# First attention stage: the additive band mask moves from identity products on TensorE into a VectorE add that copies the scores to SBUF

## The chip, the core and the metric

The kernel runs on one core of one Trainium2 chip. The metric is the device time of one execution of the whole program in microseconds (us), as the median of the runs. The program is a six-layer decoder (two attention-like mixers, two cross attentions, a mixture of experts, a binarised feed-forward); only its first layer is touched here.

## The reference, cut to what matters

The touched layer is a windowed self attention with rotary positions, 8 batches of 256 tokens, 16 heads of 64. Every query sees only keys at a distance of at most 64.

```
Q = (x @ Wq).reshape(Bx, Tx, H, D).transpose(0, 2, 1, 3)
K = (x @ Wk).reshape(Bx, Tx, H, D).transpose(0, 2, 1, 3)
V = (x @ Wv).reshape(Bx, Tx, H, D).transpose(0, 2, 1, 3)
Q = Q * cos + rotate_half(Q) * sin
K = K * cos + rotate_half(K) * sin
scores = jnp.einsum('bhqd,bhkd->bhqk', Q, K) / jnp.sqrt(jnp.float32(D))
w = Tx // 4
allowed = jnp.abs(idx[:, None] - idx[None, :]) <= w
scores = jnp.where(allowed[None, None], scores, -jnp.inf)
attn = jax.nn.softmax(scores, axis=-1)
out = jnp.einsum('bhqk,bhkd->bhqd', attn, V)
return out.transpose(0, 2, 1, 3).reshape(Bx, Tx, H * D) @ Wo
...
x = _layernorm(x + _L0_attn_ref(x, L0_attn_Wq, L0_attn_Wk, L0_attn_Wv, L0_attn_Wo), axis=-1)
```

## The kernel before

The layer is the function `window_attention`. Nothing schedules it: each engine has a written-out list of instructions, and semaphores tie the lists together. All engines work in order within their own list, so the position of a step in a list decides what is queued behind it.

A batch is worked in four **groups** (`g` = 0 to 3) of four heads (`GH` = 4). Because of the window, the 128 queries of a tile `t` need only `SPAN` = 192 keys, so one head's scores for both tiles are 2 x 192 = 384 columns of one PSUM bank, `s_bank[i]`. There is one such bank for each head of a group, and one name for all of them in the profile: `wa_scores`.

What a group's work is, by engine:

- TensorE, in `score` (lines 639 to 658): four products of a bf16 identity with the bf16 `band` (L649) write 0 or -1e30 into the 384 columns of each bank, and sixteen products of rotated q and k (L655) accumulate onto that.
- VectorE, in `maximum` (L468): for each of the four heads one reduction over 384 columns of PSUM, which gives the negated row maximum.
- ScalarE, in `exponential` (L383): two exponentials per head, of 192 columns each, which read the same PSUM bank and write `probs` to SBUF.
- TensorE turns the probabilities (`turn_probs`, L667), for two heads at a time; one such pair is a unit `u`. ScalarE takes the high half out of PSUM (`wa_pth`, L394) and VectorE the rest (`wa_ptl`, L509); TensorE weighs the values (`weigh`, L685); VectorE normalises (L494, L502).

Beside this a group carries part of the **next** batch or of the previous one:

- All groups but those of the last batch project q and k for the next batch (`project`, L596) into `s_bank[0]` and `s_bank[1]`, which VectorE reads with the cosines and sines (L462, L463) before GpSimd adds (L342, L343). So group `g+1`'s scores wait in `score` until VectorE has read the projections of group `g` (`rope_read`).
- Groups 0 and 3 (**value groups** below) make two value products each for the next batch in the single bank `m_bank` (L617, `wa_misc`). ScalarE copies the first out after its eight exponentials (L399), VectorE takes the rest (L474, `value_low`), and only then may TensorE start the second (semaphore `misc_free`).
- Groups 1 and 2 (**mix groups**) do the output projection of the previous batch there (L634) and its residual and statistics on VectorE (L482, L145 to L150).
- At the end of group 3 VectorE also applies the layer norm (L159) and splits the next input (L452).

The first batch has no previous batch and the last one has no next, so batch 0's groups 1 and 2 have no mix, and the last batch's groups have neither values nor projections. That leaves 14 value groups: two in each of batches 0 to 6.

VectorE's list in a group is: four maxima, normalise the previous unit, the value rest or the residual, `wa_ptl` of the first unit, the second value rest, four reads of the projections, `wa_ptl` of the second unit, normalise. TensorE's is: weigh the previous unit, value product or mix, turn the first unit, second value product, project, turn, weigh, turn the heads (L627), next group's scores.

Of the kernel before, what the change touches and what calls it, by code (L numbers as in the profile page):

```python
# [21 lines left out]
BF16 = mybir.dt.bfloat16  # L22
I32 = mybir.dt.int32
ALU = mybir.AluOpType
ACT = mybir.ActivationFunctionType
AX = mybir.AxisListType

P = 128
# [3 lines left out]
TPB = SEQ // P  # L32
# [77 lines left out]
def identity(pool, tile, made, done):  # L110

    pool.memset(tile[:], 0.0).then_inc(made, 1)
    pool.wait_ge(made, done)
    return pool.affine_select(out=tile[:], in_=tile[:], compare_op=ALU.not_equal, fill=1.0, base=0,
                              pattern=[[-1, P]], channel_multiplier=1)
# [47 lines left out]
def first(b):  # L163

    return isinstance(b, int) and b == 0
# [6 lines left out]
WINDOW = SEQ // 4  # L172
SPAN = P + WINDOW
# [3 lines left out]
GROUPS = 4  # L177
# [32 lines left out]
def window_attention(nc, x_dram, xt_dram, wqkv_dram, wo_dram, rope_dram, ident, half, X, next_loads):  # L210
    with ExitStack() as ctx:
        def sb(name, shape, dt=F32):
            return ctx.enter_context(nc.sbuf_tensor("wa_" + name, shape, dt))

        def sem(name):
            sems.append(nc.alloc_semaphore("wa_" + name))
            return sems[-1]
# [14 lines left out]
        vh = [sb(f"vh{k}", [P, TPB, HEADS, HD + 1], F16) for k in range(2)]  # L232
        vl = [sb(f"vl{k}", [P, TPB, HEADS, HD + 1], F16) for k in range(2)]
        probs = [sb(f"probs{k}", [P, 2, SEQ]) for k in range(4)]
        minus_top = sb("minus_top", [P, 2, GH, 2])
        pth = [sb(f"pth{k}", [P, 2 * SEQ], F16) for k in range(4)]
        ptl = [sb(f"ptl{k}", [P, 2 * SEQ], F16) for k in range(4)]
        inv = sb("inv", [P, 2, TPB, 2])
        heads_out = sb("heads_out", [P, TPB, HEADS, HD])
        heads_t = [sb(f"heads_t{k}", [P, HEADS // 2, SEQ]) for k in range(2)]  # L240
        ident_bf = sb("ident_bf", [P, P], BF16)
        band = sb("band", [P, TPB, SPAN], BF16)

        s_bank = [ctx.enter_context(nc.psum_tensor(f"wa_scores{k}", [P, 2 * SEQ], F32)) for k in range(GH)]
        t_bank = [ctx.enter_context(nc.psum_tensor(f"wa_turned{k}", [P, 512], F32)) for k in range(2)]
# [19 lines left out]
        misc_free = sem("misc_free")  # L265
        v_high = sem("v_high")
        scores = sem("scores")
        maxed = sem("maxed")
        exped = sem("exped")
        probs_t = sem("probs_t")  # L270
# [50 lines left out]
        @block.gpsimd  # L321
        def _(pool):
            identity(pool, ident, consts, 1).then_inc(consts, 1)
            identity(pool, ident_bf, consts, 3).then_inc(consts, 1)
            pool.memset(half[:], -0.5).then_inc(consts, 1)
            pool.memset(band[:], 0.0).then_inc(consts, 1)
            pool.wait_ge(consts, 6)

            for t, base in ((0, 0), (1, P - WINDOW)):
                n = 6 + 2 * t  # L330
                pool.affine_select(out=band[:, t], in_=band[:, t], compare_op=ALU.is_ge, fill=NEG,
                                   base=base + WINDOW, pattern=[[-1, SPAN]], channel_multiplier=1).then_inc(consts, 1)
                pool.wait_ge(consts, n + 1)
                pool.affine_select(out=band[:, t], in_=band[:, t], compare_op=ALU.is_ge, fill=NEG,
                                   base=WINDOW - base, pattern=[[1, SPAN]], channel_multiplier=-1).then_inc(consts, 1)

            def rotate(b, par, g, w):

                n = rope_count(b, g, w)
                pool.wait_ge(rope_read, n + 1)  # L340
                out = turned[w][par]
                pool.tensor_tensor(out[:, g, 0], by_cos[w][:, 0], by_sin[w][:, 1], ALU.add)  # L342
                pool.tensor_tensor(out[:, g, 1], by_cos[w][:, 1], by_sin[w][:, 0], ALU.add).then_inc(rope_done, 1)  # L343

            def batch(b, par, before=True, after=True):
                for g in range(GROUPS):
                    if after:
                        for w in range(2):
                            rotate(b + 1, 1 - par, g, w)
                    if before and g == 2:  # L350
                        norm.root(pool, b - 1, 0)
                        norm.root(pool, b - 1, 1)

            for g in range(GROUPS):
                for w in range(2):
                    rotate(0, 0, g, w)
            pool.wait_ge(w_low, 6)
            batch(0, 0, before=False)
            with pool.Fori(0, BATCH // 2 - 1) as i:
                batch(2 * i + 1, 1)  # L360
                batch(2 * i + 2, 0)
            batch(BATCH - 1, 1, after=False)
            norm.root(pool, BATCH - 1, 0)
            norm.root(pool, BATCH - 1, 1)

        @block.scalar
        def _(act):
# [8 lines left out]
            def exponential(b, g, i):  # L376
                n = GH * (GROUPS * b + g) + i
                u, h = 2 * g + i // 2, i % 2
                act.wait_ge(maxed, n + 1)
                if not (first(b) and u < 2):  # L380
                    act.wait_ge(probs_t, b * 16 + 2 * u - 2)
                for t in range(TPB):
                    ins = act.activation(probs[2 * (u % 2) + t][:, h, t * WINDOW:t * WINDOW + SPAN],  # L383
                                         s_bank[i][:, t * SPAN:(t + 1) * SPAN], ACT.Exp,
                                         bias=minus_top[:, g % 2, i, t:t + 1])
                ins.then_inc(exped, 1)

# [55 lines left out]
        def _(dve):  # L443
# [21 lines left out]
            def maximum(b, g, i):  # L465
                n = GH * (GROUPS * b + g) + i
                dve.wait_ge(scores, GROUPS * b + g + 1)
                dve.tensor_reduce(minus_top[:, g % 2, i], s_bank[i][:, 0:2 * SPAN].rearrange("p (t s) -> p t s", t=2),  # L468
                                  AX.X, ALU.max, negate=True).then_inc(maxed, 1)

            def value_low(b, par, i, n):
                t, c = divmod(i, 2)
# [75 lines left out]
            split_w(0)  # L548
            split_w(1)
            dve.wait_ge(rope_loaded, 32)  # L550
            for g in range(GROUPS):
                rope(0, g, 0)
                rope(0, g, 1)
                if g < 2:
                    split_w(g + 2)
                elif g == 2:
                    split_w(4)
                    split_w(5)
# [18 lines left out]
        def _(pe):  # L577
            def project(b, par, g, w):

                n = rope_count(b, g, w)  # L580
                if w == 0:
                    pe.wait_ge(x_low, b + 1)
                    if first(b):
                        pe.wait_ge(w_low, g + 1)
                if first(b):
                    if g >= 2:
                        pe.wait_ge(rope_read, n - 3)
                else:
                    pe.wait_ge(exped, GH * (GROUPS * (b - 1) + g) + w + 1)
                bank = rope_bank(b, g, w)  # L590
                for a in range(2):
                    cols = slice(g * 512 + w * 256 + a * P, g * 512 + w * 256 + (a + 1) * P)
                    m = 0
                    for k in range(KT_):
                        for weight, x in ((wh, xh), (wh, xl), (wl, xh)):
                            ins = pe.matmul(bank[:, a * SEQ:(a + 1) * SEQ], weight[:, k, cols], x[:, par, k],  # L596
                                            start=(m == 0), stop=(m == 3 * KT_ - 1))
                            m += 1
                ins.then_inc(projected, 1)
# [38 lines left out]
            def score(b, par, g):  # L638

                pe.wait_ge(rope_done, rope_count(b, g, 1) + 1)  # L640
                if not (first(b) and g == 0):
                    pe.wait_ge(exped, GH * (GROUPS * b + g))
                if isinstance(b, int) and b == BATCH - 1:
                    pe.wait_ge(rope_read, 2 * GROUPS * BATCH)
                else:
                    pe.wait_ge(rope_read, 2 * GROUPS * (b + 1) + 2 * g)
                q, k = turned[0][par], turned[1][par]
                for i in range(GH):
                    pe.matmul(s_bank[i][:, 0:2 * SPAN], ident_bf[:], band[:].rearrange("p t s -> p (t s)"),  # L649
                              start=True, stop=False, skip_group_check=True)  # L650
                for part in range(2):
                    for t in range(TPB):
                        for i in range(GH):
                            rows = slice(FREQS * i, FREQS * (i + 1))
                            ins = pe.matmul(s_bank[i][:, t * SPAN:(t + 1) * SPAN], q[rows, g, part, t * P:(t + 1) * P],  # L655
                                            k[rows, g, part, t * WINDOW:t * WINDOW + SPAN], start=False,
                                            stop=(part == 1 and t == TPB - 1), skip_group_check=True)
                ins.then_inc(scores, 1)

            def turn_probs(b, u):  # L660
# [54 lines left out]
                    elif after:  # L715
                        score(b + 1, 1 - par, 0)

            pe.wait_ge(consts, 10)
            for g in range(GROUPS):
                project(0, 0, g, 0)  # L720
                project(0, 0, g, 1)
# [2079 lines left out]
```

## Time and profile before

| | before |
|---|---|
| median of 3 runs | 1324.53 us |
| the 3 runs | 1319.22, 1324.74, 1324.53 us |
| the profiled execution | 1319.36 us |
| its span | 1317.6 us |
| TensorE busy | 1104.7 us, 84% of the span |
| VectorE busy | 940.1 us, 71% |
| ScalarE busy | 702.1 us, 53% |
| GpSimd busy | 389.0 us, 30% |
| mean granted TensorE clock | 0.927 of 2.4 GHz |

The busy times cover the whole program. The touched layer fills the first 442 us. In it the profile's rows are to be read by group: a group begins when VectorE starts the first of its four L468 reductions.

### The profile page before, as it was taken

How to read it: one execution, taken by the hardware profiler on the slowest of the kernel's cores; microseconds unless marked ns; L12 is line 12 of the kernel's file. 1: busy time of each engine (PE TensorE's matmuls, PEld its weight loads, DVE VectorE, ACT ScalarE, POOL GpSimd, SP SyncE). 2: the span in 40 equal slices, each digit the busy share in tenths (PEclk: the TensorE clock that was granted, in tenths of full speed). 3: DMA queues.
4: the chain of work that ended last, by engine and by line, in shares of the span. 5: the costliest groups of instructions: out<-in, count | busy, mean ns of one | idle time of the engine just before them, and what ended most of it. 6: DMA issues, size and time to landing. Idle time of an engine off the chain costs nothing. (4 is left out here: it accounts for less than half of the span.)

```text
span 1317.6 us, 29952 instructions
## 1 busy us (share of the span) xinstructions
PE 1104.7 (84%) x10635; PEld 895.0 (68%) x10635; DVE 940.1 (71%) x2221; ACT 702.1 (53%) x1458; POOL 389.0 (30%) x538
## 2 busy tenths in 40 slices
PE   5899989989988699996449999489999569999696
PEld 3578768768777477775337777378888447777485
DVE  7676766767765279885847884569998528898487
ACT  2444444444444155553727776267778525655484
POOL 5122222212220155552050000413421125555232
PEclk9999999999999799997559999699999769999799
DMA  6000000100000500002443531300100000000011
GB/s 255 1 10 2 10 10 1 68 3 1 2 1 2 182 13 22 21 8 119 192 146 114 209 118 40 123 21 17 32 8 9 0 24 20 14 21 8 33 49 48
DMA packets 34064, 65.26 MB, mean 50 GB/s; under 512 B 7590, under 2 KB 23334, under 8 KB 30886
## 3 DMA queue, kind: packets, MB, share of 16 engines
q1 hardware_dynamic: 32422, 59.62, 12.8%
q0 software_dynamic: 1536, 4.20, 0.9%
q8 instruction: 70, 1.15, 0.4%
q14 instruction: 36, 0.29, 0.1%
HBM read 43.03 MB, written 12.39 MB: 42 GB/s over the span
## 5 line engine op out<-in xcount | busy, mean ns | idle before, releaser
L925 POOL TENSOR_TENSOR ca_z<-ca_z,ca_top 128x308 f32<-128x308 f32 x128 | 92.5, 723 | 135.4 <-DVE ca_top L1054 135.1
L383 ACT ACTIVATE wa_probs<-wa_scores,wa_minus_top 128x192 f32<-128x192 f32 x256 | 83.1, 436 | 68.2 <-DVE wa_minus_top L468 68.2
L394 ACT ACTIVATE wa_pth<-wa_turned 128x384 f16<-128x384 f32 x128 | 58.2, 505 | 96.9 <-PE wa_turned L667 96.9
L997 ACT ACTIVATE ca_pth<-ca_turned 77x512 f16<-77x512 f32 x128 | 75.8, 592 | 61.5 <-PE ca_turned L1181 60.9
L342 POOL TENSOR_TENSOR wa_q<-wa_by_cos,wa_by_sin 128x256 f32<-128x256 f32 x32 | 23.4, 730 | 284.2 <-DVE wa_by_sin L463 284.2
L1181 PE MATMUL ca_turned<-ident,ca_probs 128*77 128x128 f32 x512 | 85.0, 290 | 20.8 <-ACT ca_probs L989 19.8
L1172 PE MATMUL ca_scores<-ca_km,ca_q 128*128 128x308 f32 x256 | 91.0, 439 | 6.0 <-ACT ca_q L970 5.7
L468 DVE TENSOR_REDUCE wa_minus_top<-wa_scores 128x2 f32<-128x384 f32 x128 | 62.4, 550 | 37.7 <-PE wa_scores L655 37.7
L1059 DVE SCALAR_TENSOR_TENSOR ca_ptl<-ca_turned,ca_pth 77x512 f16<-77x512 f32 x128 | 86.7, 677 | 2.6 <-ACT ca_pth L997 2.6
L989 ACT ACTIVATE ca_probs<-ca_z 128x308 f32<-128x308 f32 x128 | 58.2, 454 | 44.8 <-POOL ca_z L925 43.8
L596 PE MATMUL wa_scores<-wa_xh,wa_wh 128*128 128x256 f16 x256 | 70.9, 277 | 10.8 <-DVE wa_wl L447 8.9
L1181 PEld LDWEIGHTS ca_turned<-ident,ca_probs 128*77 128x77 f32 x512 | 56.7, 150 | 26.6 <-ACT ca_probs L989 23.0
L667 PE MATMUL wa_turned<-ident,wa_probs 128*128 128x128 f32 x512 | 67.8, 274 | 8.0 <-DVE wa_ptl L509 5.4
L596 PE MATMUL wa_scores<-wa_xl,wa_wh 128*128 128x256 f16 x256 | 70.9, 277 | 0.0
L596 PE MATMUL wa_scores<-wa_xh,wa_wl 128*128 128x256 f16 x256 | 70.9, 277 | 0.0
L2357 PE MATMUL re_g<-re_convh,re_w_gh 128*128 128x256 f16 x256 | 69.8, 273 | 1.2 <-DVE re_convl L2252 1.2
L509 DVE SCALAR_TENSOR_TENSOR wa_ptl<-wa_turned,wa_pth 128x384 f16<-128x384 f32 x128 | 65.0, 549 | 7.9 <-ACT wa_pth L394 7.9
L2357 PE MATMUL re_g<-re_convl,re_w_gh 128*128 128x256 f16 x256 | 69.8, 273 | 0.0
L2357 PE MATMUL re_g<-re_convh,re_w_gl 128*128 128x256 f16 x256 | 69.8, 273 | 0.0
L2341 PE MATMUL re_in<-re_xt,re_w_in 128*128 128x256 f32 x256 | 61.8, 403 | 9.0 <-ACT re_xt L2122 9.0
L667 PEld LDWEIGHTS wa_turned<-ident,wa_probs 128*128 128x128 f32 x512 | 58.2, 141 | 15.2 <-issue 6.3
L2341 PEld LDWEIGHTS re_in<-re_xt,re_w_in 128*128 128x128 f32 x256 | 51.1, 202 | 18.8 <-issue 7.2
(325 smaller groups left out, 3613.0 us busy)
## 6 DMA issues: line engine op xcount, KB each, us to landing
ex_stage<-in_ew SPq DMA_DIRECT2D x16, 1024.0 KB, 6.9
slots<-slots_zeros SPq DMA_DIRECT2D x10, 512.0 KB, 5.8
ca_xs<-tokens SPq DMA_DIRECT2D x16, 256.0 KB, 2.3
ex_xe<-slots SPq DMA_DIRECT2D x11, 320.0 KB, 3.2
slots<-ex_y SPq DMA_DIRECT2D x9, 320.0 KB
wa_x_stage<-in_xt SPq DMA_DIRECT2D x8, 256.0 KB, 3.0
tokens<-in_x SPq DMA_DIRECT2D x1, 2048.0 KB, 14.8
ca_w<-in_xw SPq DMA_DIRECT2D x2, 1024.0 KB, 5.7
```

The lines of the kernel that those rows point to most:

```text
L383: ins = act.activation(probs[2 * (u % 2) + t][:, h, t * WINDOW:t * WINDOW + SPAN], s_bank[i][:, t * SPAN:(t + 1) * SPAN], ACT.Exp, bias=mi ...
L468: dve.tensor_reduce(minus_top[:, g % 2, i], s_bank[i][:, 0:2 * SPAN].rearrange("p (t s) -> p t s", t=2), AX.X, ALU.max, negate=True).then_ ...
L509: dve.scalar_tensor_tensor(out=spans(ptl[k][:]), in0=spans(t_bank[h][:]), scalar=PSCALE, in1=spans(pth[k][:]), op0=ALU.mult, op1=ALU.subtr ...
L596: ins = pe.matmul(bank[:, a * SEQ:(a + 1) * SEQ], weight[:, k, cols], x[:, par, k], start=(m == 0), stop=(m == 3 * KT_ - 1))
L667: ins = pe.transpose(t_bank[h][:, j * SEQ + t * P:j * SEQ + (t + 1) * P], probs[2 * (u % 2) + t][:, h, j * P:(j + 1) * P], ident[:])
L925: pool.tensor_tensor(z[k][:], z[k][:], top[:, k].unsqueeze(2).broadcast_to((P, UH, CTX)), ALU.subtract).then_inc(shift, 1)
L997: act.activation(pth[k][0:CTX], t_bank[k][0:CTX], ACT.Copy, scale=PSCALE).then_inc(probs_high, 1)
L1059: dve.scalar_tensor_tensor(out=ptl[k][0:CTX], in0=t_bank[k][0:CTX], scalar=PSCALE, in1=pth[k][0:CTX], op0=ALU.mult, op1=ALU.subtract).then ...
L1172: pe.matmul(s_bank[c % 2][:, 0:UH * CTX], q[par][:, g, t * P:(t + 1) * P], km[par][:, g, h:h + UH].rearrange("p h k -> p (h k)"), start=Tr ...
L1181: ins = pe.transpose(t_bank[k][0:CTX, h * P:(h + 1) * P], probs[k][:, h], ident[:])
L2341: ins = pe.matmul(i_bank[s % 2][:, k], w_in[:, g, m * P:(m + 1) * P], xt[:, g], start=(g == 0), stop=(g == KT_ - 1))
L2357: ins = pe.matmul(g_bank[m][:, k], w[:, j, cols], x[par][:, j], start=(n == 0), stop=(n == 3 * HT - 1))
```

## The change

The band is no longer written into PSUM by TensorE. The four identity products of each group are gone, and with them the bf16 identity. The band is now an f32 tile. VectorE adds it to each head's 384 score columns while it copies them to a new SBUF tile `z[i]`, one for each head of a group, and the reduction reads `z[i]`. ScalarE's exponentials read `z[i]` as well. A new semaphore `masked` counts the adds: the reduction waits for its own add, and TensorE's reuse of the score banks waits for the add, where it used to wait for the exponential. The add waits until the previous group's exponential of the same head has read `z[i]`. TensorE's sixteen score products go by tile and then by part, where they went by part and then by tile; the first part now starts the accumulation.

```diff
+        z = [sb(f"z{i}", [P, TPB, SPAN]) for i in range(GH)]
...
-        ident_bf = sb("ident_bf", [P, P], BF16)
-        band = sb("band", [P, TPB, SPAN], BF16)
+        band = sb("band", [P, TPB, SPAN])
...
                     ins = act.activation(probs[2 * (u % 2) + t][:, h, t * WINDOW:t * WINDOW + SPAN],
-                                         s_bank[i][:, t * SPAN:(t + 1) * SPAN], ACT.Exp,
+                                         z[i][:, t], ACT.Exp,
                                          bias=minus_top[:, g % 2, i, t:t + 1])
...
             def maximum(b, g, i):
                 n = GH * (GROUPS * b + g) + i
                 dve.wait_ge(scores, GROUPS * b + g + 1)
-                dve.tensor_reduce(minus_top[:, g % 2, i], s_bank[i][:, 0:2 * SPAN].rearrange("p (t s) -> p t s", t=2),
-                                  AX.X, ALU.max, negate=True).then_inc(maxed, 1)
+                if not (first(b) and g == 0):
+                    dve.wait_ge(exped, n - GH + 1)
+                dve.tensor_tensor(z[i][:], s_bank[i][:, 0:2 * SPAN].rearrange("p (t s) -> p t s", t=2), band[:],
+                                  ALU.add).then_inc(masked, 1)
+                dve.wait_ge(masked, n + 1)
+                dve.tensor_reduce(minus_top[:, g % 2, i], z[i][:], AX.X, ALU.max, negate=True).then_inc(maxed, 1)
...
-                    pe.wait_ge(exped, GH * (GROUPS * (b - 1) + g) + w + 1)
+                    pe.wait_ge(masked, GH * (GROUPS * (b - 1) + g) + w + 1)
...
-                    pe.wait_ge(exped, GH * (GROUPS * b + g))
+                    pe.wait_ge(masked, GH * (GROUPS * b + g))
...
-                for i in range(GH):
-                    pe.matmul(s_bank[i][:, 0:2 * SPAN], ident_bf[:], band[:].rearrange("p t s -> p (t s)"),
-                              start=True, stop=False, skip_group_check=True)
-                for part in range(2):
-                    for t in range(TPB):
+                for t in range(TPB):
+                    for part in range(2):
                         for i in range(GH):
                             rows = slice(FREQS * i, FREQS * (i + 1))
                             ins = pe.matmul(s_bank[i][:, t * SPAN:(t + 1) * SPAN], q[rows, g, part, t * P:(t + 1) * P],
-                                            k[rows, g, part, t * WINDOW:t * WINDOW + SPAN], start=False,
-                                            stop=(part == 1 and t == TPB - 1), skip_group_check=True)
+                                            k[rows, g, part, t * WINDOW:t * WINDOW + SPAN],
+                                            start=(part == 0), stop=(part == 1))
```

The rest of the diff renumbers the semaphore that counts the constants.

The order of VectorE (DVE) in batch 0, group 3, a value group, before. A row is a line of the kernel, the operation, its output and inputs, and the semaphores that it waits for; `wa_minus_top` is the negated maximum, `wa_vl` the value rest.

```order
L468 TENSOR_REDUCE wa_minus_top<-wa_scores 128x2 [waits wa_scores] x4
L494 RECIPROCAL wa_inv<-wa_out 128x4 [waits wa_normed,wa_weighted]
L502 TENSOR_TENSOR wa_heads_out<-wa_out,wa_inv 128x2x128 [waits wa_inverted]
L474 SCALAR_TENSOR_TENSOR wa_vl<-wa_misc,wa_vh 128x8x64 [waits wa_v_high]
L509 SCALAR_TENSOR_TENSOR wa_ptl<-wa_turned,wa_pth 128x2x192 [waits wa_probs_high] x2
```

The same place in the changed kernel; the first two rows stand four times in turn.

```order
L470 TENSOR_TENSOR wa_z<-wa_scores,wa_band 128x384 [waits wa_exped,wa_scores]
L473 TENSOR_REDUCE wa_minus_top<-wa_z 128x2 [waits wa_masked]
...
L498 RECIPROCAL wa_inv<-wa_out 128x4 [waits wa_normed,wa_weighted]
L506 TENSOR_TENSOR wa_heads_out<-wa_out,wa_inv 128x2x128 [waits wa_inverted]
L478 SCALAR_TENSOR_TENSOR wa_vl<-wa_misc,wa_vh 128x8x64 [waits wa_v_high]
L513 SCALAR_TENSOR_TENSOR wa_ptl<-wa_turned,wa_pth 128x2x192 [waits wa_probs_high] x2
```

Four instructions have become eight, each reduction behind a wait for the add ahead of it, and all that follows stands behind them.

The order of TensorE (PE) at the end of a group of batch 0, before: the turned heads, the scores of the next group, and the first product of `weigh`.

```order
L627 MATMUL wa_misc<-ident,wa_heads_out 128x128 x3
L649 MATMUL wa_scores<-wa_band,wa_ident_bf 128x384 [waits wa_rope_read,wa_exped,wa_rope_done]
L649 MATMUL wa_scores<-wa_band,wa_ident_bf 128x384 x3
L655 MATMUL wa_scores<-wa_k,wa_q 128x192 x16
L685 MATMUL wa_out<-wa_vh,wa_pth 128x65 [waits wa_normed,wa_probs_low]
```

The same place in the changed kernel.

```order
L632 MATMUL wa_misc<-ident,wa_heads_out 128x128 x3
L657 MATMUL wa_scores<-wa_k,wa_q 128x192 [waits wa_rope_read,wa_masked,wa_rope_done]
L657 MATMUL wa_scores<-wa_k,wa_q 128x192 x15
L687 MATMUL wa_out<-wa_vh,wa_pth 128x65 [waits wa_normed,wa_probs_low]
```

Four products are gone from every group, and the first score product carries their waits.

## Rows read from the trace of the kernel before

**Rows 1.** Windows of a batch's groups: us; busy PE, PEld, DVE, ACT, POOL; clock; DMA.

```profile
201.10:213.20 12.10, 12.10 (x149) 10.67 (x148) 8.45 (x22) 4.94 (x13) 2.78 (x4) 1.00 0.01 3
...
225.31:238.17 12.86, 11.34 (x145) 8.77 (x144) 9.98 (x22) 6.43 (x16) 2.79 (x4) 1.00 0.01 1
238.17:251.12 12.95, 11.34 (x145) 8.77 (x143) 8.74 (x19) 5.96 (x15) 2.79 (x4) 1.00 0.49 172
```

**Rows 2.** Timeline of TensorE: start, duration, operation, count, idle time before.

```profile
201.71 3.70 PE L634 MATMUL wa_misc<-wa_wo,wa_heads_t 128*128 128x256 f32 x16
210.81 0.81 PE L649 MATMUL wa_scores<-wa_band,wa_ident_bf 128*128 128x384 bf16 x4
211.55 1.58 PE L655 MATMUL wa_scores<-wa_k,wa_q 32*128 32x192 f32 x32
227.21 1.04 PE L667 MATMUL wa_turned<-ident,wa_probs 128*128 128x128 f32 x8
229.77 0.39 PE L617 MATMUL wa_misc<-wa_wh,wa_xh 128*128 128x512 f16 x1 [1.52 <-DVE wa_vl L474]
```

**Rows 3.** Timeline of VectorE, a mix group and a value group.

```profile
201.10 1.95 DVE L468 TENSOR_REDUCE wa_minus_top<-wa_scores 128x2 f32<-128x384 f32 x4 [1.42 <-PE wa_scores L655]
206.03 0.43 DVE L145 BATCH_NORM_STATS2 wa_stats<-wa_res 128x6 f32<-128x256 f32 x1
206.50 0.18 DVE L148 BATCH_NORM_AGGREGATE wa_mv<-wa_stats 128x2 f32<-128x6 f32 x1
...
225.31 1.95 DVE L468 TENSOR_REDUCE wa_minus_top<-wa_scores 128x2 f32<-128x384 f32 x4 [1.42 <-PE wa_scores L655]
...
229.02 0.69 DVE L474 SCALAR_TENSOR_TENSOR wa_vl<-wa_misc,wa_vh 128x512 f16<-128x512 f32 x1 [1.21 <-ACT wa_vh L399]
...
237.32 0.68 DVE L452 SCALAR_TENSOR_TENSOR wa_xl<-wa_x_stage,wa_xh 128x512 f16<-128x512 f32 x1
```

**Rows 4.** Timeline of ScalarE in the same value group.

```profile
225.90 2.60 ACT L383 ACTIVATE wa_probs<-wa_scores,wa_minus_top 128x192 f32<-128x192 f32 x8 [2.19 <-DVE wa_minus_top L468]
228.34 0.65 ACT L399 ACTIVATE wa_vh<-wa_misc 128x512 f16<-128x512 f32 x1
```

**Rows 5.** Groups of instructions by line: shapes, count, busy us, mean ns, idle before.

```profile
L468 DVE TENSOR_REDUCE wa_minus_top<-wa_scores 128x2 f32<-128x384 f32 x128 | 62.4, 550 | 37.7 <-PE wa_scores L655 37.7
L509 DVE SCALAR_TENSOR_TENSOR wa_ptl<-wa_turned,wa_pth 128x384 f16<-128x384 f32 x128 | 65.0, 549 | 7.9 <-ACT wa_pth L394 7.9
...
L1054 DVE TENSOR_REDUCE ca_top<-ca_z 128x4 f32<-128x308 f32 x128 | 58.8, 459 | 0.1
L1048 DVE TENSOR_TENSOR ca_z<-ca_scores,ca_limit 128x308 f32<-128x308 f32 x64 | 30.4, 475 | 19.9 <-PE ca_scores L1172 17.5 <-ACT ca_probs L989 1.4 <-issue 0.3
```

**Rows 6.** Timeline of VectorE in batch 0 and in the last batch.

```profile
54.17 1.95 DVE L468 TENSOR_REDUCE wa_minus_top<-wa_scores 128x2 f32<-128x384 f32 x4 [1.06 <-PE wa_scores L655]
57.77 1.02 DVE L509 SCALAR_TENSOR_TENSOR wa_ptl<-wa_turned,wa_pth 128x384 f16<-128x384 f32 x2 [1.10 <-ACT wa_pth L394]
...
389.65 1.95 DVE L468 TENSOR_REDUCE wa_minus_top<-wa_scores 128x2 f32<-128x384 f32 x4 [0.85 <-PE wa_scores L655]
393.26 1.02 DVE L509 SCALAR_TENSOR_TENSOR wa_ptl<-wa_turned,wa_pth 128x384 f16<-128x384 f32 x2 [1.10 <-ACT wa_pth L394]
```

**Rows 7.** Windows around changes of the granted clock, columns as in rows 1.

```profile
34.00:38.00 4.00, 1.49 (x7) 0.53 (x8) 1.39 (x2) 0.90 (x2) 0.00 (x0) 1.00 0.00 0
...
426.50:430.00 3.50, 1.66 (x30) 1.22 (x28) 1.82 (x7) 0.96 (x2) 0.00 (x0) 0.99 0.00 0
430.00:433.30 3.30, 3.02 (x7) 2.48 (x8) 0.00 (x0) 0.23 (x1) 0.00 (x0) 0.50 0.00 0
453.80:457.20 3.40, 1.30 (x4) 0.68 (x4) 3.00 (x6) 0.26 (x1) 0.04 (x1) 1.00 1.09 381
457.20:464.00 6.80, 5.59 (x21) 4.79 (x22) 2.19 (x5) 2.86 (x7) 2.06 (x3) 0.50 0.64 221
```

**Rows 8.** Timeline of TensorE: the last batch's first mix.

```profile
430.28 5.23 PE L634 MATMUL wa_misc<-wa_wo,wa_heads_t 128*128 128x256 f32 x16 [0.69 <-ACT wa_heads_t L404]
```

More of the change, by code:

```diff
@@ L267, in window_attention @@
         scores = sem("scores")
+        masked = sem("masked")
         maxed = sem("maxed")
@@ L323, in _ @@
             identity(pool, ident, consts, 1).then_inc(consts, 1)
-            identity(pool, ident_bf, consts, 3).then_inc(consts, 1)
             pool.memset(half[:], -0.5).then_inc(consts, 1)
             pool.memset(band[:], 0.0).then_inc(consts, 1)
-            pool.wait_ge(consts, 6)
+            pool.wait_ge(consts, 4)
             for t, base in ((0, 0), (1, P - WINDOW)):
-                n = 6 + 2 * t
+                n = 4 + 2 * t
                 pool.affine_select(out=band[:, t], in_=band[:, t], compare_op=ALU.is_ge, fill=NEG,
@@ L550, in _ @@
             dve.wait_ge(rope_loaded, 32)
+            dve.wait_ge(consts, 8)
             for g in range(GROUPS):
@@ L716, in batch @@
                         score(b + 1, 1 - par, 0)
-            pe.wait_ge(consts, 10)
+            pe.wait_ge(consts, 2)
             for g in range(GROUPS):
```

## The prediction, on record before the result was known

> **What bounds the kernel now.** I read four views: the windows of one batch's groups, the timelines of TensorE, VectorE and ScalarE inside them, the groups of instructions by line for prices, and windows where the granted clock changes. The windows show which engine has room: in a mix group TensorE is busy 12.10 of 12.10 us and VectorE 8.45, in the value groups TensorE 11.34 of 12.86 and 12.95 us, VectorE 9.98 and 8.74 [rows 1]. The middle row dots a second mix group, of 12.11 us. So a batch takes 50.02 us; mix groups are bound by TensorE alone, while value groups contain one wait: TensorE stands 1.52 us ahead of the second value product until VectorE has taken the value rest [rows 2]. What ends last there is a chain over three engines: four maxima, eight exponentials, value copy, value rest, second value product. VectorE starts its maxima at 225.31, the exponentials start at 225.90, the value copy at 228.34, the rest at 229.02, the second product at 229.77 [rows 2 to 4]. Whatever the change saves in a mix group is real; whatever lengthens the maxima in a value group is real too.
>
> **What is removed.** Four identity products per group: from the start of the first to the start of the score products, 211.55 - 210.81 = 0.74 us [rows 2]. In every group they stand directly ahead of the scores, with nothing beside them on TensorE, so the scores come 0.74 us sooner wherever TensorE is late. There are 32 groups, so at most 32 x 0.74 = 23.7 us. The exponential's hold on the score banks goes as well; since the exponentials end at 225.90 + 2.60 = 228.50 and the next scores are ready at 238.17 [rows 1, 4], that is worth nothing. The reordering of the sixteen score products changes neither their number nor their banks' rotation: nothing.
>
> **What is added on VectorE.** Four adds of 128x384 per group from PSUM and SBUF. The trace has the same shape with such operands: L509, 549 ns, while L1048 with 308 columns takes 475 [rows 5]. I take 0.55. The four reductions now follow a wait each. Before, they started (1.95 - 0.55) / 3 = 0.467 us apart [rows 3]; a reduction behind an add of its own cannot overlap it. An instruction that waits for its predecessor's result started 206.50 - 206.03 - 0.43 = 0.04 us after its end [rows 3]. One head thus costs 0.55 + 0.04 + 0.467 = 1.06 us, four 4.23, against 4 x 0.467 = 1.87: VectorE has 2.36 us more per group. Bounds: from below 2 x 0.40 per head (384 columns in the pitch that the rows leave after some 0.07 of start), if the pair overlapped fully, 3.2 in all; from above 2 x 0.55 + 2 x 0.04 = 1.18 per head, 4.7 in all. I take 4.23, since the dependence is in the code and the gap in the rows.
>
> The reduction now reads SBUF. The trace has one from SBUF: L1054, 459 ns for 308 columns; 76 columns more at about 1.04 ns (0.40 us / 384) make 538, against 550 from PSUM [rows 5]. So 0.01 us, which I leave out. The Trainium skill (page "VectorE: DVE Perf Modes", section on the TRN2 errata) gives a VectorE operation 58 cycles of fixed cost from SBUF and 120 from PSUM, which would be 65 ns less per reduction. By that rule the value groups' delay below would be about 0.26 us shorter, some 4 us over the stage; the trace's two reductions don't bear it out. ScalarE's exponentials from SBUF I cost like those from PSUM: only the last pair is on the chain.
>
> **Mix groups (12, plus the last batch's two).** The mix itself keeps TensorE busy for 3.70 us [rows 2] while the maxima run, and the first unit's exponentials are out before it ends. What comes later on VectorE (residual, `wa_ptl`) TensorE needs only behind both projections. VectorE's 8.45 + 2.36 = 10.8 us fit in 12.10 - 0.74 = 11.36 [rows 1]. Each is 0.74 us shorter. Cover gone: were VectorE's list another 0.55 us longer, the next scores would wait for its projection reads, and the gain would shrink by all that goes beyond.
>
> **Value groups (14).** The fourth maximum comes at 3 x 1.057 + 0.59 + 0.55 = 4.31 us after the group's start. ScalarE was behind its eight exponentials before and is now fed by the maxima: the last pair starts at 4.35, and at a pitch of (228.34 - 225.90) / 8 = 0.305 us the value copy starts at 4.96, where it was 228.34 - 225.31 = 3.03 [rows 4]. Everything behind it (value rest, second value product, project, turn, weigh, heads) shifts by 1.93 us as one piece. Less 0.74 the next scores come 1.19 us later. In group 3 VectorE itself is later still: its list ends with norm and split, 237.32 + 0.61 = 237.93, only 0.24 ahead of 238.17 [rows 1, 3]. It gets the full 1.93, so the period grows by 1.93 - 0.24 = 1.69. Its 0.61 is 0.68 less the overlap of 0.07 that such operations have. Group 0 has no such tail and grows by 1.2. A steady batch: 1.2 + 1.7 - 2 x 0.74 = +1.4 us.
>
> **The ends.** In batch 0's groups 1 and 2 and the last batch's group 0, without mix, `wa_ptl` starts 3.60 us after the group, directly behind ScalarE's exponentials [rows 6]; it shifts by 1.93 too, and after the earlier scores each group grows by about 1.1. Batch 0: -0.74 (first scores) + 1.2 + 2 x 1.1 + 1.5 = +4.1. Last batch: +1.2, two mix groups at 0.5 - 0.74 = -0.24 each, and +1.9 in group 3, which has no scores to win from: +2.6. Batch 6 has no split, so its group 3 gives 0.5 back. Sum: 4.1 + 6 x 1.4 - 0.5 + 2.6 = **+14.6 us**.
>
> **The clock.** In a value group TensorE's standing time grows. The first turn started 1.90 us after the group and took 1.04, the second value product came at 4.46 [rows 2]; that product now comes at 6.39. Of the 4.5 us between, the turns, now one by one behind the exponentials of each head, keep TensorE busy for 1.04 to 1.2. The rows show what the granted clock did around such stretches: after 1.66 busy of 3.50 us it went to 0.50 for 3.3 us, after 1.30 of 3.40 to 0.50 for 6.8 us, while after 1.49 of 4.00 at 34 us it stayed at 1.00 [rows 7]. In a value group before, only 1.52 us in one piece were idle and the clock stayed 1.00 [rows 1]. The price: the last batch's mix took 5.23 us where the low clock covered 3.0 of it, and 3.70 at the high one: 1.5 us [rows 2, 8]. A whole covered stretch of 3.3 us costs half of it, 1.65; one of 6.8 us with 5.59 busy costs 2.8 [rows 7]. I take 11 of the 14 value groups, eight at 1.65 and three at 2.8, which is 21.6, less 4 for the groups 3 where VectorE is 0.5 us later than TensorE anyway: **+17 us**. Bounds: 0, and 14 x 2.8 = 39. The Trainium skill warns of this pattern (page "TensorE: Matmul & The Clock Gate", section "HAM oscillation"): waits between bursts of products throttle the array again in each turn of a loop. By that rule every value group would pay, by the rows above 14 x 1.65 = 23; it speaks against this change.
>
> **Sum.** 1319.4 + 14.6 + 17 = 1351.0 against the profiled execution. The runs of before lie in two places, 1319.2 and 1324.6, and their median is 5.2 above the profiled one; I add half of that, 2.6: **1353.6 us**.
>
> **Rivals.**
> (A) The clock holds, as in the row at 34 us: only the +14.6, 1336.6. For it: that row, and the clock of 1.00 all through rows 1. Against: twice in rows 7 it fell after stretches no emptier than these.
> (B) The clock falls in every value group and stays low for the longer time: 1322 + 14.6 + 39 = 1376. For it: the row of 6.8 us. Against: behind the gap come 24 dense products, and the row of 3.3 us had such work.
> (C) Faster. VectorE's add and reduction overlap. The delay of the value copy is 3 times the head's cost less 1.24; gain and loss of a steady batch cancel when that delay is about 1.2, so when a head costs 0.81 us. Below it the mix groups' 0.74 wins; with the value groups' wait hidden as well the whole 23.7 us come back, 1322 - 23.7 = 1298. For it: 0.40 us of streaming per instruction. Against: the `masked` wait between them, and 0.04 us seen after such waits.
> (D) No change: both sides cancel, at 0.81 us per head and a clock that holds, 1324.
>
> **How the numbers follow.** Forecast 0.53, A 0.25, B 0.09, C 0.05, D 0.08. The forecast's own range is 1344 to 1364 (the clock term from 8 to 27 within its bounds). For 8 in 10 I take in A and stop short of B and C: 1331 to 1370. About 0.5% (6.6 us) is what a measurement can tell. Faster has C's 0.05, within 0.5% D's 0.08 and a little of A, 0.1 in all, and slower the rest, 0.85.
>
> **What would show it.** Right: adds of 0.55 us and a pitch of 1.06 per head; value rest 5.6 us after the group's start; TensorE's idle ahead of the second value product grown from 1.5 towards 2.9; mix groups of 11.4 us; windows of 0.50 clock between 60 and 430 us, which did not exist. Wrong: a head's pitch under 0.9, a clock of 1.00 throughout (then A), scores that wait for the projection reads in mix groups (then more than B), or another time behind the first layer.

## The result, and the profile after

The changed kernel takes 1359.74 us (median of 4 runs, 1359.42 to 1359.81) against 1321.88 us before (median of 4, 1316.64 to 1324.74). The ratio is 1.0291, with a 95% interval of 1.0252 to 1.0329: slower by 2.9%. The forecast was 1353.6 us in a range of 1331 to 1370.

The windows of one batch show where it went. They answer to [rows 1]; columns are the same: the window, then busy TensorE, its weight loads, VectorE, ScalarE, GpSimd, the granted clock, DMA. The first two are mix groups, the last two the value groups 3 and 0.

```profile
223.31:234.76 11.45, 11.45 (x147) 10.31 (x143) 10.57 (x25) 5.42 (x13) 2.79 (x4) 1.00 0.01 1
234.76:246.22 11.46, 11.46 (x147) 10.32 (x143) 10.57 (x25) 5.42 (x13) 3.17 (x5) 1.00 0.01 1
246.22:263.44 17.22, 14.10 (x153) 9.63 (x150) 12.17 (x25) 7.03 (x16) 3.44 (x6) 0.80 0.01 2
263.44:280.29 16.85, 13.43 (x133) 9.01 (x130) 11.01 (x24) 6.57 (x15) 2.79 (x4) 0.80 0.37 132
```

Mix groups went from 12.10 to 11.45 us, with TensorE still busy throughout; VectorE's work rose by 2.1 us in them and cost nothing. The two value groups shown went from 12.86 and 12.95 to about 17 us, and the clock, 1.00 in every value group before, reads 0.80. Over all 14 value groups the mean went from 13.1 to 16.1 us; the shortest after the change is the one whose clock stayed at 1.00, with 14.24 us. TensorE's busy time *rose* in the two from 11.3 to 14.1 and 13.4 us although it has less to do: the same products at the low clock take longer.

VectorE's timeline at the start of a value group (of batch 3; start, duration, operation, idle time before) answers to [rows 3], ScalarE's to [rows 4]:

```profile
209.06 0.56 DVE L470 TENSOR_TENSOR wa_z<-wa_scores,wa_band 128x384 f32<-128x384 f32 x1 [2.33 <-issue]
209.65 0.55 DVE L473 TENSOR_REDUCE wa_minus_top<-wa_z 128x2 f32<-128x384 f32 x1
210.12 0.55 DVE L470 TENSOR_TENSOR wa_z<-wa_scores,wa_band 128x384 f32<-128x384 f32 x1
...
212.81 0.55 DVE L473 TENSOR_REDUCE wa_minus_top<-wa_z 128x2 f32<-128x384 f32 x1
213.28 0.17 DVE L498 RECIPROCAL wa_inv<-wa_out 128x4 f32<-128x4 f32 x1
...
214.71 0.69 DVE L478 SCALAR_TENSOR_TENSOR wa_vl<-wa_misc,wa_vh 128x512 f16<-128x512 f32 x1 [0.71 <-ACT wa_vh L399]
```

```profile
213.40 0.80 ACT L383 ACTIVATE wa_probs<-wa_z,wa_minus_top 128x192 f32<-128x192 f32 x2 [0.25 <-DVE wa_minus_top L473]
214.10 0.58 ACT L399 ACTIVATE wa_vh<-wa_misc 128x512 f16<-128x512 f32 x1
```

A head costs 210.12 - 209.06 = 1.06 us, and the value rest starts 214.71 - 209.06 = 5.65 us into the group, where it was 229.02 - 225.31 = 3.71. Between its exponentials ScalarE now waits for maxima.

The next view is TensorE in the value group that starts at 246.22, and the clock beside it:

```profile
249.31 0.66 PE L669 MATMUL wa_turned<-ident,wa_probs 128*128 128x128 f32 x4 [0.33 <-ACT wa_probs L383]
252.62 0.61 PE L622 MATMUL wa_misc<-wa_wh,wa_xh 128*128 128x512 f16 x1 [2.66 <-DVE wa_vl L478]
253.02 0.63 PE L622 MATMUL wa_misc<-wa_wl,wa_xh 128*128 128x512 f16 x1
253.45 0.63 PE L622 MATMUL wa_misc<-wa_wh,wa_xl 128*128 128x512 f16 x1
```

```profile
248.20:252.60 4.40, 1.31 (x8) 0.84 (x8) 3.49 (x9) 3.65 (x10) 0.00 (x0) 0.85 0.00 0
252.60:256.00 3.40, 3.38 (x10) 1.49 (x11) 0.89 (x2) 0.60 (x1) 0.00 (x0) 0.50 0.00 0
256.00:259.30 3.30, 3.30 (x23) 2.57 (x21) 1.95 (x3) 0.00 (x0) 0.00 (x0) 0.68 0.00 0
259.30:263.40 4.10, 4.10 (x85) 3.69 (x84) 3.89 (x10) 1.99 (x4) 2.79 (x4) 1.00 0.01 4
```

TensorE is idle for 2.66 us ahead of the second value product (1.52 before, [rows 2]) and was busy for 1.31 of the 4.40 us from 248.20 on. Then the clock is at 0.50 just as the dense part of the group begins: the 512-column products start 0.43 us apart (253.45 - 253.02); in the first value product of the same group, at the high clock, they started 0.22 us apart (247.38 - 247.16). It is the picture of [rows 7], in nearly every value group.

All 32 groups of both profiled executions, summed by kind (from one first VectorE step to the next), give the books:

| part of the first layer | before, us | after, us | difference |
|---|---|---|---|
| up to the first group | 41.75 | 43.93 | +2.2 |
| 14 value groups | 183.5 | 225.2 | +41.8 |
| 12 mix groups of batches 1 to 6 | 145.3 | 137.5 | -7.8 |
| batch 0, groups 1 and 2 | 19.2 | 21.5 | +2.3 |
| last batch, groups 0, 1, 2 | 30.4 | 33.3 | +2.9 |
| last group and end of the layer | 22.2 | 24.4 | +2.2 |
| sum, first layer | 442.3 | 485.9 | +43.6 |
| everything behind it | 875.3 | 872.1 | -3.2 |

The whole loss, and more, is in 14 of 32 groups. In 13 of them the clock was low for part of the time, in five for about 7 us. Not every fall costs time: in group 0 of batch 3 the clock was low from 210.3 to 213.7, all of it ahead of the second value product's start at 215.46. TensorE's wait there shrank to 1.42 us, and the group took 14.25 us.

The 2.2 us at the front are not the change's. The clock of the window 20 to 44 us was 0.93, 0.79 or 0.72 from kernel to kernel, and the first group started between 40.7 and 44.8 us accordingly: it was 0.72 in the control below, which leaves the prologue as it was, and 0.93 in the changed kernel with the early copy, whose first group started at 40.87. The code behind the layer is the same in all kernels, and took from 871.8 to 875.5 us in the twelve profiles; so the -3.2 is not put down to the change either.

### The profile page after: what moved, and what is told of

Same layout as the page of the kernel before. It is cut to its first block and busy times, and to the rows that moved or that the text cites. A ratio compares the mean times of both kernels' runs of the same rounds, so it can differ in the third digit from the quotient of the medians.

```text
span 1358.0 us, 30009 instructions
## 1 busy us (share of the span) xinstructions
PE 1117.0 (82%) x10507; PEld 894.6 (66%) x10507; DVE 1008.8 (74%) x2349; ACT 720.3 (53%) x1458; POOL 389.3 (29%) x536
## 5 line engine op out<-in xcount | busy, mean ns | idle before, releaser
L383 ACT ACTIVATE wa_probs<-wa_z,wa_minus_top 128x192 f32<-128x192 f32 x256 | 102.4, 447 | 98.0 <-DVE wa_minus_top L473 98.0
L669 PE MATMUL wa_turned<-ident,wa_probs 128*128 128x128 f32 x512 | 74.3, 285 | 21.5 <-ACT wa_probs L383 12.9
L470 DVE TENSOR_TENSOR wa_z<-wa_scores,wa_band 128x384 f32<-128x384 f32 x128 | 70.4, 550 | 20.6 <-PE wa_scores L657 18.2
L601 PE MATMUL wa_scores<-wa_xh,wa_wh 128*128 128x256 f16 x256 | 75.6, 295 | 11.3 <-DVE wa_wl L447 9.3
L601 PE MATMUL wa_scores<-wa_xl,wa_wh 128*128 128x256 f16 x256 | 75.1, 293 | 0.0
L601 PE MATMUL wa_scores<-wa_xh,wa_wl 128*128 128x256 f16 x256 | 74.4, 291 | 0.0
L473 DVE TENSOR_REDUCE wa_minus_top<-wa_z 128x2 f32<-128x384 f32 x128 | 70.8, 553 | 4.4
```

The costliest lines, as they stand in the source:

```text
L470: dve.tensor_tensor(z[i][:], s_bank[i][:, 0:2 * SPAN].rearrange("p (t s) -> p t s", t=2), band[:], ALU.add).then_inc(masked, 1)
L473: dve.tensor_reduce(minus_top[:, g % 2, i], z[i][:], AX.X, ALU.max, negate=True).then_inc(maxed, 1)
L669: ins = pe.transpose(t_bank[h][:, j * SEQ + t * P:j * SEQ + (t + 1) * P], probs[2 * (u % 2) + t][:, h, j * P:(j + 1) * P], ident[:])
```

## The experiments

All medians are compared with runs of the kernel before on the same chip.

**The removal alone.** The identity products go, and nothing takes their place, so this kernel applies no mask:

```diff
-                for i in range(GH):
-                    pe.matmul(s_bank[i][:, 0:2 * SPAN], ident_bf[:], band[:].rearrange("p t s -> p (t s)"),
-                              start=True, stop=False, skip_group_check=True)
```

> The kernel before without the identity products and with no add in their place, so no band mask is applied at all (that part of the computation is left out): the removal alone. My theory: each of the 32 score steps comes 0.74 us sooner, and only in the seven groups 3 of batches 0 to 6 does VectorE's tail swallow some 0.5 us of it: about -21 us, 1301 us against a median of 1322 before. Rival (the products stood beside other work, or TensorE does not bound the mix groups): less than -8 us.

Measured: 1302.83 us against 1321.21, ratio 0.987 (0.9821 to 0.992). The windows are value group 0 and mix group 1 of batch 4:

```profile
228.98:241.28 12.30, 10.49 (x130) 7.91 (x127) 8.73 (x20) 5.97 (x15) 2.78 (x4) 1.00 0.51 181
241.28:252.73 11.45, 11.45 (x144) 10.32 (x143) 8.45 (x21) 4.94 (x13) 2.78 (x4) 1.00 0.01 1
```

Both are 0.65 us shorter, and group 3 took 12.61 instead of 12.86, as VectorE's tail allows. So the saving is real and on the path, in nearly all groups. The rival falls. (In three groups of this profile the clock fell where it had not before, so the 18.4 us are what is left of the saving.)

**The addition alone.** The identity products stay; VectorE adds a tile of zeros (`band32`) and all reads go to `z`:

```diff
+                dve.tensor_tensor(z[i][:], s_bank[i][:, 0:2 * SPAN].rearrange("p (t s) -> p t s", t=2), band32[:],
+                                  ALU.add).then_inc(masked, 1)
```

> The identity products stay, and VectorE also copies the scores to z with an add (of a tile of zeros), reduces z, and the exponentials read z: the addition alone. My theory: mix groups keep their 12.1 us, the 14 value groups grow by 1.9 us each (27), the groups without mix by 1.9 (some 8 in all), and the clock falls in nearly every value group as in the changed kernel (some 24): about +59 us, 1381 us. The two parts would then add up to what the change did. Rival 1, without a clock effect: +35 us, 1357. Rival 2, VectorE's 75 us of added work counts in full: +75 us, 1397.

Measured: 1377.78 us, ratio 1.0426 (1.0374 to 1.0478), +56.6 us. Value group 0, mix group 1 and value group 3 of batch 1:

```profile
103.34:118.24 14.90, 11.77 (x146) 8.66 (x143) 10.94 (x22) 6.57 (x15) 2.79 (x4) 1.00 0.07 20
118.24:130.34 12.10, 12.10 (x151) 10.67 (x147) 10.57 (x25) 5.43 (x13) 2.78 (x4) 1.00 0.01 3
142.45:159.02 16.57, 13.44 (x147) 9.19 (x144) 12.20 (x25) 7.03 (x16) 2.79 (x5) 0.90 0.01 1
```

The mix group takes 12.10 us to the hundredth as before, with 2.1 us more on VectorE. The value group without a low clock takes 14.90, 1.95 more than 12.95. Its clock fell in 10 of the 14 value groups. The two parts give -18.4 + 56.6 = +38.2, the change gave +37.9: they add up, within intervals of some 7 us for each part.

**The clock held up.** In the gap of each value group, in the changed kernel:

```diff
+            def keep_busy(b, g, n):
+                pe.wait_ge(masked, GH * (GROUPS * b + g) + 1)
+                for _ in range(n):
+                    pe.matmul(s_bank[0][:, 0:SEQ], wh[:, 0, 0:P], xh[:, 0, 0], start=True, stop=True)
```

> The changed kernel with 20 products (128x256, f16, result unused, into the bank that the next projection overwrites) between the turn of the first unit and the second value product in each of the 14 value groups, where TensorE stands idle; at 0.11 us each they take 2.1 of the 2.8 idle us. My theory: the clock stays at 1.00 in the value groups, their periods become 14.2 (group 0) and 14.6 us (group 3), and the clock's share of the loss goes: about 1338 us, 22 under the changed kernel. Rival (the low clock is a mere symptom and the chain over VectorE and ScalarE sets the time in any case): 1360 or a little more.

Measured: 1338.63 us, ratio 1.0125 (1.0078 to 1.0172): 21.1 us under the changed kernel, by work that computes nothing. Groups 3 and 0, the counterparts of the 17.22 and 16.85 above:

```profile
237.62:252.16 14.54, 13.60 (x172) 10.53 (x169) 12.11 (x25) 7.04 (x16) 3.44 (x6) 1.00 0.01 2
252.16:266.41 14.25, 13.01 (x153) 9.95 (x150) 10.95 (x24) 6.57 (x15) 2.78 (x4) 1.00 0.46 157
```

The clock is 1.00 and the periods are those that the chain alone gives (forecast: 14.55 and 14.2); of the 20.1 us between the two profiled executions 19.2 lie in the value groups. The clock fell in only two value groups and the last batch's first. The low clock is a cause, not a symptom, and it made more than half of the loss.

**The control.** The same filling, 10 products, in the kernel before (`pe.wait_ge(exped, ...)` in place of `masked`).

> The control for the filled one: the kernel before with 10 such products in the same place, 1.1 of its 1.5 idle us. Both theories: no change, 1322 within 3 us, since the clock was at 1.00 there already. If it gains or loses more, filling does something other than hold the clock.

Measured: 1326.68 us, ratio 1.0041 (1.0019 to 1.0064): 5.5 us slower, outside the 3 us expected. Its groups keep their periods to a hundredth, 12.95 and 12.86, but two don't, one of them this (group 0 of batch 3; the row of the kernel before stands first, from its own profile):

```profile
186.21:201.10 14.89, 11.47 (x145) 8.91 (x146) 8.83 (x19) 6.11 (x15) 2.79 (x4) 1.00 0.07 21
```

```profile
188.66:207.68 19.02, 15.23 (x155) 11.49 (x156) 9.02 (x19) 6.31 (x15) 2.79 (x4) 0.82 0.05 16
```

These are groups 0 of batches 3 and 5, the two places where the loop over batches jumps back (it has three turns of two batches; at its end, ahead of batch 7, no such pause stands). TensorE pauses there in every kernel without waiting for anything that the profile shows, for 2.5 to 4.5 us. In the kernel before the clock stayed at 1.00 behind both pauses. In the filled kernel it went to 0.50 at 192.5, 1.3 us after this one, and a second pause followed:

```profile
191.24 0.20 PE L690 MATMUL wa_out<-wa_vh,wa_pth 128*128 128x65 f16 x1 [2.64 <-issue]
194.58 0.59 PE L617 MATMUL wa_misc<-wa_wl,wa_xh 128*128 128x512 f16 x1 [1.22 <-issue]
```

Of the 7.5 us between the two profiled executions, 6.5 lie in these two groups, 2.4 ahead of the first group, and the end of the layer gives 1.5 back. So filling is neutral in the other 12 value groups, and the excess does not come from them. What the pauses are, and whether the filling has a part in the falls behind them, I did not test.

**The order of adds and maxima.** In the filled kernel:

```diff
+                if i == 0:
+                    mask(b, g, 0)
+                if i < GH - 1:
+                    mask(b, g, i + 1)
                 dve.wait_ge(masked, n + 1)
                 dve.tensor_reduce(minus_top[:, g % 2, i], z[i][:], AX.X, ALU.max, negate=True).then_inc(maxed, 1)
```

> The changed kernel with the filling products (which held the clock in all but three groups), and VectorE's list staggered: add 0, add 1, maximum 0, add 2, maximum 1, add 3, maximum 2, maximum 3, so that no reduction stands directly behind the add that it waits for. My theory (a head costs 1.06 us because of that wait, and the value groups follow the fourth maximum): eight instructions at 0.47 us, fourth maximum at 3.8 instead of 4.3 us, value groups shorter by 0.48 us each and the groups without mix too, mix groups the same: some 8 us under the filled one, 1330. Rival (the wait between add and maximum costs nothing that matters): 1338.

Measured: 1333.15 us against 1324.75, ratio 1.0062 (1.004 to 1.0083), some 8 us less than the filled one by the ratios (0.0063 of 1322). But the two intervals still touch, and its profile shows value groups only 0.28 us shorter (13.96 and 14.27), not 0.48. Of the 8.2 us by which the layer ended sooner in the two profiles, 4.4 lie in the value groups and 3.4 ahead of the first group, which are not the stagger's; so of the 8 us only about half is shown. VectorE did what was forecast (the fourth maximum came 3.8 us into the group); ScalarE took over the bound:

```profile
250.88 0.78 ACT L383 ACTIVATE wa_probs<-wa_z,wa_minus_top 128x192 f32<-128x192 f32 x2
251.57 0.57 ACT L399 ACTIVATE wa_vh<-wa_misc 128x512 f16<-128x512 f32 x1
```

Its exponentials from SBUF start (251.57 - 250.88) / 2 = 0.35 us apart; from PSUM it was 0.305 [rows 4].

**VectorE in the mix groups only.**

```diff
+        def by_vector(b, g):
+            return not first(b) and g in (1, 2)
```

> VectorE adds the band in the mix groups of batches 1 to 7 only, where TensorE is the bound and VectorE has room; the other 18 groups keep TensorE's identity products. My theory: each score step of a mix group comes 0.65 to 0.74 us sooner and nothing else moves (the last batch gives half of it back): -9 us, 1312 against 1321. Rival (the adds cost in mix groups too, by ports or by VectorE's list): no change or slower.

Measured: 1316.03 us against 1324.75, ratio 0.9932 (0.9911 to 0.9952). Groups 0, 1 and 2 of batch 4:

```profile
238.31:250.72 12.41, 10.80 (x144) 8.52 (x143) 8.73 (x19) 5.98 (x15) 2.79 (x4) 1.00 0.51 180
250.72:262.17 11.45, 11.45 (x147) 10.32 (x143) 10.57 (x25) 5.43 (x13) 2.79 (x4) 1.00 0.00 1
262.17:274.19 12.02, 12.02 (x148) 10.59 (x145) 10.57 (x26) 5.42 (x13) 3.73 (x6) 1.00 0.01 1
```

A group is shorter by more than a tenth of a microsecond only where the *next* group's scores come without identity products. The adds themselves cost nothing in these groups; group 2 of the last batch took 11.19 instead of 10.78 us.

**The chain, tested without the change.** In the kernel before, ScalarE's value copy moves up, and VectorE's `layer_norm` steps of group 3 move ahead of the second value rest:

```diff
                     for i in range(GH):
                         exponential(b, g, i)
-                    if after and g in (0, 3):
-                        value(b + 1, 1 - par, g // 3 * 2, steps["value", g // 3 * 2])
+                        if after and g in (0, 3) and i == 1:
+                            value(b + 1, 1 - par, g // 3 * 2, steps["value", g // 3 * 2])
```

> The kernel before, with two moves and no change in the mask: ScalarE copies the first value product after four of the eight exponentials instead of after all eight, and VectorE's two layer norm steps of group 3 stand before the second value rest instead of at the group's end. It tests the chain named for the value groups without touching the change. My theory: the value rest comes about 1.0 us sooner, group 0 takes 11.9 instead of 12.95 us, group 3 about 12.0 instead of 12.86: some -13 us, 1308. Rival (value groups bound by something else): no change.

Measured: 1313.82 us, ratio 0.9908 (0.9887 to 0.993). Value groups 3 and 0:

```profile
121.74:133.62 11.88, 11.33 (x145) 8.78 (x144) 9.96 (x22) 6.55 (x16) 2.79 (x4) 1.00 0.01 1
133.62:145.51 11.89, 11.34 (x145) 8.79 (x144) 8.83 (x19) 6.09 (x15) 2.78 (x4) 1.00 0.08 24
```

They are 0.98 and 1.06 us shorter with the same work. The chain of maxima, exponentials, value copy, value rest and second product is what set them; group 0, which has no layer norm, shows it for the copy alone. The time fell by 10.9 us where 13 were expected; the two groups behind the loop's jumps took 18.36 and 17.02 us in its profile, with a low clock, against 14.89 and 14.49 before.

**Both together.**

> Both: the add on VectorE in the mix groups only, and the early value copy with the layer norm moved. My theory: the two gains lie in different groups and add up: -22 us, 1299 against 1321.

Measured: 1300.72 us against 1324.75, ratio 0.982 (0.9797 to 0.9843): 1.8% faster than before, 4.6% than the changed kernel by the two ratios (0.982 / 1.0291). It is below both of its parts, 1316.03 and 1313.82.

**The changed kernel with the early copy.**

> The changed kernel (all groups add on VectorE, no filling products) with the early value copy and the layer norm moved. My theory: the copy no longer waits for the fourth maximum, only VectorE's own list does: value rest 4.8 instead of 5.65 us into the group, so 0.9 us less per value group and another 0.5 in groups 3: some -15 us, 1345 against 1360; more if the shorter gap lets the clock stay up in some groups. Rival (the whole loss sits in VectorE's list): 1360.

Measured: 1334.91 us against 1323.0, ratio 1.0096 (1.0065 to 1.0127): 10 us better than expected. The value rest starts 4.86 us into the group, as expected, behind VectorE's own list:

```profile
88.06 0.55 DVE L470 TENSOR_TENSOR wa_z<-wa_scores,wa_band 128x384 f32<-128x384 f32 x1
...
92.58 0.42 DVE L506 TENSOR_TENSOR wa_heads_out<-wa_out,wa_inv 128x256 f32<-128x256 f32 x1
92.92 0.68 DVE L478 SCALAR_TENSOR_TENSOR wa_vl<-wa_misc,wa_vh 128x512 f16<-128x512 f32 x1
```

In batches 1 to 6 the value groups without a fall took 13.25 to 13.46 us, 0.8 to 1.1 less than with the clock held and the late copy, which is the expected gain of the chain. The surplus goes with the clock: in the profiled execution (the fastest of the seven) it fell in seven value groups instead of 13, in none of them for 7 us. TensorE's wait ahead of the second value product was 1.77 us there instead of 2.66, so 0.9 us less of it went with half of the falls.

**All three mends on the changed kernel** (early copy, stagger, 10 filling products).

> The changed kernel with all three mends: early value copy and layer norm moved, staggered adds and maxima, and 10 filling products in the gap of the value groups. My theory: second value product 5.0 us into the group (4.5 before the change, 6.4 with it), value groups of about 12.7 us, mix groups 11.45 us: 1313 to 1316 against 1322, so a gain from the same change, though less than with VectorE in the mix groups only. Rival (75 us of added VectorE work must show somewhere): 1335 or more.

Measured: 1319.53 us against 1323.0, ratio 0.997 (0.9947 to 0.9993). The value groups took 12.84 and 12.96 us, near the forecast 12.7, the mix groups 11.45; the groups behind the loop's jumps took 13.58 (after a group 3 of 15.72) and 17.87 us. With these three mends the change breaks even with the kernel before. But the early copy does not need the change: alone it gave 0.9908, so against a kernel that has it the add in every group still costs some 0.6% (0.997 / 0.9908), the other two mends included, where the add in the mix groups only gains 0.9% (0.982 / 0.9908).

## Why the prediction was right, point by point

- **What bounds the groups**: right. Mix groups follow TensorE (removal alone: 12.10 to 11.45 us; addition alone: 12.10 again). Value groups follow the named chain (early copy: 12.95 to 11.89).
- **The 0.74 us per group**: mis-sized, it is 0.65. The score products used to start behind the identity products; now they start 289.99 - 289.43 = 0.56 us after the turned heads, where the identity products started 222.92 - 222.45 = 0.47 after them and the scores 0.74 behind those. The saving is 0.47 + 0.74 - 0.56 = 0.65:

```profile
289.43 0.63 PE L632 MATMUL wa_misc<-ident,wa_heads_out 128*128 128x128 f32 x4
289.99 1.58 PE L657 MATMUL wa_scores<-wa_k,wa_q 32*128 32x192 f32 x32
```

- **VectorE's 1.06 us per head**: right (1.06), and the value rest at 5.65 against 5.64.
- **The reduction from SBUF**: 553 ns against 550 from PSUM for the same shape, where 538 was forecast. The Trainium skill's lower fixed cost for VectorE from SBUF ("VectorE: DVE Perf Modes", section on the TRN2 errata) does not show here.
- **Exponentials from SBUF cost like those from PSUM**: an assumption that was wrong, though it weighs little. They last 447 instead of 436 ns but follow each other at 0.35 instead of 0.305 us. In the changed kernel only the last pair counts (value copy at 5.04 instead of the forecast 4.96 us). The same table of the Trainium skill's page gives ScalarE more fixed cost from SBUF than from PSUM (224 against 172 cycles); here the trace agrees in the sign.
- **Value groups**: 14.25 and 14.54 us with the clock held, forecast +1.2 and +1.7, so right. A steady batch lost 1.7 us by the chain (14.25 + 14.54 + 11.45 + 11.46 against 50.02), not 1.4, mostly through the smaller 0.65.
- **The clock**: the mechanism right, the size too small. The forecast was 17 us from eleven falls, three of them long. There were 13, five long, and the filling gave back 21.1 us. The 4 us that the forecast took off, because VectorE is later than TensorE in groups 3, were not there: a long fall cost 2.6 and 2.7 us in two groups 3 (17.15 and 17.22 against 14.55) and 2.5 to 2.6 in the groups 0. Against that, the short fall in group 0 of batch 3 cost nothing, which the forecast did not have.
- **Sum**: 14.6 + 17 = 31.6 forecast; by the runs, 17.4 for the chain (1338.63 against 1321.21, three falls still in it) and 21.1 for the clock. Both terms were too small, so the forecast's 1353.6 lies 6.1 us under the 1359.74. Rival A (clock holds) gave 1336.6, and the kernel with the clock held measured 1338.63.
- **Rivals B, C, D** did not occur: no head under 1.0 us (C), no cancelling, since the value groups lost 3.0 us each on average against 0.65 won in a mix group (D), and not all falls long (B), though B had the number of falls, all 14, nearer than the forecast's eleven.

## What to carry to other kernels

Here, work moved from the engine that bounds one stage to one that has room there was a gain only in stages where the receiving engine stood in no chain. Look at each kind of stage, and where they differ, move it only in those that gain. A small wait added to TensorE in a loop can cost more by its clock than by its length: with 1.1 us more of waiting a value group lost up to 2.7 us by the clock, on top of what the chain took. Try a mend on the kernel before as well, or its gain is put down to the change. And where an engine waits for a result that passes through a third one, look at what stands ahead of it in that third list; here moving one copy ahead of the last four exponentials, with VectorE's list to match, took 1.0 us from a value group, more than the 0.65 that the identity products cost.

## What the runs showed of the hardware that was not expected

- ScalarE's exponentials of 128x192 start 0.305 us apart from PSUM and 0.35 from SBUF, while their recorded durations differ by only 0.011. Pitch, not duration, is what a chain pays.
- In the changed kernel some 3.4 us at the low clock cost a value group 3 1.5 to 1.7 us (15.64 to 16.13 against the 14.15 to 14.55 of the same groups with the clock held), and some 7 us cost 2.5 to 2.7 (17.22 against 14.54, 16.85 against 14.25). They cost nothing where they lay ahead of the end of TensorE's wait (group 0 of batch 3, 14.25 us at a mean clock of 0.88).
- Filling TensorE's gap with 20 unused products of 128x256 in each value group made the changed kernel 21.1 us faster.
- At both jumps back of the loop TensorE stands for 2.5 to 4.5 us in every kernel, and the groups behind them took 14.49 and 14.89 us in the kernel before, 16.86 and 19.02 in its filled copy, whose clock fell there.
